# Attention's value products: a group over all four key blocks in one go, in place of two halves four steps apart

## The chip, the cores and the metric

The kernel runs on one core of one Trainium2 chip. The metric is the device time of one execution in microseconds (us), of which the median over the runs is taken.

## The reference

Three layers follow each other on x of 8 images by 512 tokens by 128 features: a Mamba block, then a mixture of experts, then attention, then the mixture of experts again. The change is in attention, which computes, cut to what matters:

```python
qk = x @ W_qk;  q, k = split(qk);  v = x @ W_v          # 8 heads, 64 wide (q, k) and 16 wide (v)
dots = einsum('bhid,bhjd->bhij', q, k) * SCALE          # per head 512 x 512
attn = softmax(dots + bias[None], axis=-1)              # bias by the clipped distance of j and i
out  = einsum('bhij,bhjd->bhid', attn, v)               # the value products
return out @ W_out + b_out
```

## The kernel before

All is in float32. An image's attention is done in `ST` = 32 steps. A step is one head and one block of 128 queries (`head_of`): its scores against all 512 keys are two records of 64x512 on TensorE (L1879, into `at_p_scores`, three banks; issued in pairs, two steps ahead). VectorE adds the band of biases and finds the row minimum (L2124, "bias(s)" below), ScalarE takes the exponential (L2011, "exp(s)"), TensorE turns the 128x512 probabilities by four 128x128 transposes (L1886, "turn(s)", into `at_p_probs_T`, two banks), and a copy puts them in `at_probs_T` (even steps VectorE L2133, odd steps ScalarE L1978, "take(s)").

Eight steps make a group `v` (4 heads of one half of the heads, two query blocks). For a group the value products (`values`, L1908) run on TensorE: for each of the 4 key blocks `j` and 4 heads `q` one product with a 128x32 weight (the 16 values, a one for the row sum, and zeros) against 128x256 probabilities, accumulated over `j` in `at_p_o_T`. The four heads write four groups of 32 partitions. Each product makes two records in the trace. `valued` is raised at the end of a group.

Nothing is planned at run time: each engine's queue is the order in which its block of the program is written. In each step TensorE issues the scores of steps s+2 and s+3 (even s), value products if the step has any, then `tail` (the output side of the image before: `turn_back`, L1917, L1930, L1936, and its router, L1298 in step 14, L1304 in step 15), turn(s), and then `head` (the input side of the next image: L1830 in step 16, projections L1836 in steps 19 to 28, the V projection L1842 in step 30). The first image has no tail, the last no head. The six images between run in a loop of three rounds of two. ScalarE's queue in an even step has exp(s), take(s-1), its tail and head; VectorE's has bias(s), take(s-2), its tail (router, layer norm) and head.

Of the kernel before, what the change touches and what calls it, by code (L numbers as in the profile page):

```python
# [16 lines left out]
TPB = T // P  # L17
# [1688 lines left out]
def attention(k, at):  # L1706
# [4 lines left out]
    NG = H // HG  # L1711
    ST = H * TPB
    VS = 2 * HG
    RING = 4
    SV = ST // VS
    k.begin_stage()
    with ExitStack() as c:
# [34 lines left out]
        turned_taken = [S("turned_taken0"), S("turned_taken1")]  # L1752
        valued, oT_ready = S("valued"), S("oT_ready")
# [9 lines left out]
        def use(slot, b, u):  # L1763

            head, tail = HEAD[slot], TAIL[slot]
            if isinstance(b, int) and b == -1:
                return u - tail + 1
            if isinstance(b, int) and b == B:
                return head - tail + (head + tail) * (B - 1) + tail + u + 1
            return head - tail + (head + tail) * b + u + 1  # L1770
# [5 lines left out]
        Q_USE, K_USE, V_USE, O_USE = (2, 4, 5, 6), (3, 3, 4, 5), 6, 2  # L1776
# [12 lines left out]
        def head_of(s):  # L1789

            gr, q = s // (ST // NG), s % HG
            it = s % (ST // NG) // VS * 2 + s % VS // HG
            return gr * HG + q, gr, q, it
# [23 lines left out]
        def _(pe):  # L1817
            k.from_one(pe, turned, valued)

            def mm_free(slot, b, u):  # L1820
                pe.wait_ge(mm_taken[slot], use(slot, b, u))

            def mm_there(slot, b, u):
                pe.wait_ge(mm_taken[slot], use(slot, b, u) + 1)
# [21 lines left out]
            def head(b, s):  # L1846

                if s == 16:
                    x_turn(b)
                elif s in (19, 23, 25, 27):  # L1850
                    p = (19, 23, 25, 27).index(s)
                    project(b, 0, Q_USE[p], p)
                elif s == 21:
                    project(b, 0, K_USE[0], H // 2)
                elif s in (24, 26, 28):
                    p = (24, 26, 28).index(s) + 1
                    project(b, 1, K_USE[p], H // 2 + p)
                elif s == 30:
                    project_v(b)

            def scores(b, par, s):

                if s == 0:
                    mm_there(0, b - 1, K_USE[0])
                elif s == 2:
                    mm_there(0, b - 1, Q_USE[1])
                    mm_there(1, b - 1, K_USE[1])
                elif s == ST // 2:
                    mm_there(0, b - 1, Q_USE[3])
                    mm_there(1, b - 1, K_USE[3])  # L1870
                for n in (s, s + 1):
                    if n >= SCB:
                        pe.wait_ge(biased, 1 + b * ST + n - SCB + 1)
                    elif not (isinstance(b, int) and b == 0):
                        before = ST - SCB + (n - ST % SCB) % SCB
                        pe.wait_ge(biased, 1 + (b - 1) * ST + before + 1)
                    hd, _, _, it = head_of(n)
                    half = slice(hd % 2 * DQK, (hd % 2 + 1) * DQK)
                    nc.tensor.matmul(psc[:, n % SCB, :], qT[par][half, hd // 2, it * P:(it + 1) * P],  # L1879
                                     kT[par][half, hd // 2, :], start=True, stop=True).then_inc(scored, 1)  # L1880

            def turn(b, s):
                pe.wait_ge(probs_ready, 1 + b * ST + s + 1)
                pe.wait_ge(turned_taken[s % 2], 1 + b * (ST // 2) + s // 2)
                for j in range(TPB):
                    mm = nc.tensor.transpose(ppt[:, s % 2, j * P:(j + 1) * P], pr[:, s % RING, j * P:(j + 1) * P],  # L1886
                                             k.ident[:])
                mm.then_inc(turned, 1)


            IDLE_BEFORE = {5: 3, 7: 3, 9: 3, 14: 14, 15: 3}
            VALUES_AT = {}
            for v, at in enumerate(((10, 14), (18, 22), (26, 30))):
                VALUES_AT.update({s: (v, 2 * j, 2 * j + 2) for j, s in enumerate(at)})

            def values(b, par, v, first, end):


                hd0, gr, _, it = head_of(v * VS)
                if first == 0:  # L1900
                    if v == 0:
                        mm_there(1, b - 1, V_USE)
                    for slot in range(2):
                        pe.wait_ge(turned_taken[slot], 1 + b * (ST // 2) + (v + 1) * (VS // 2))
                    pe.wait_ge(oT_ready, 1 + b * NG + gr)
                for j in range(first, end):
                    for q in range(HG):
                        mm = nc.tensor.matmul(pot[32 * q:32 * q + 32, it * P:(it + 2) * P], vv[par][:, j, hd0 + q, :],  # L1908
                                              prT[:, v % 2, q, j, :], start=j == 0, stop=j == TPB - 1)
                if end == TPB:  # L1910
                    mm.then_inc(valued, 1)

            def turn_back(b, gr):
                pe.wait_ge(oT_ready, 1 + (b - 1) * NG + gr + 1)
                mm_free(1, b, gr)
                for j in range(TPB):
                    mm = nc.tensor.transpose(pmm[:, 1, j * P:(j + 1) * P], oT[gr][:, j * P:(j + 1) * P], k.ident[:])  # L1917
                mm.then_inc(mm_done[1], 1)

            def tail(b, par, s):  # L1920

                if s in (1, 2):
                    values(b - 1, 1 - par, SV - 1, TPB // 2 * (s - 1), TPB // 2 * s)
                elif s in (3, 5):
                    turn_back(b, s // 2 - 1)
                elif s == 7:
                    mm_there(1, b, 1)
                    mm_free(0, b, 0)
                    for j in range(TPB):
                        mm = nc.tensor.transpose(pmm[:, 0, j * P:(j + 1) * P], on[:, j, :], k.ident[:])  # L1930
                    mm.then_inc(mm_done[0], 1)
                elif s == 9:
                    mm_there(0, b, 0)
                    mm_free(1, b, O_USE)
                    for j in range(TPB):
                        mm = nc.tensor.matmul(pmm[:, 1, j * P:(j + 1) * P], onT[:, j * P:(j + 1) * P], w_o,  # L1936
                                              start=True, stop=True)
                    mm.then_inc(mm_done[1], 1)
                elif s == 14:
                    rt.pe_turn(pe, b - 1)  # L1940
                elif s == 15:
                    rt.pe_logits(pe, b - 1)
                elif s == 20:
                    rt.pe_ranks(pe, b - 1)

            def core(b, par, first, last):
                for s in range(ST):
                    if s % 2 == 0 and s + 2 < ST:
                        scores(b, par, s + 2)
                    elif s % 2 == 0 and not last:  # L1950
                        scores(b + 1, 1 - par, s + 2 - ST)
                    if s in VALUES_AT:
                        values(b, par, *VALUES_AT[s])
                    if not first:
                        tail(b, par, s)
                    elif s + LATE < ST:
                        head(-1, s + LATE)
                    turn(b, s)
                    if not last:
                        head(b, s)  # L1960
# [15 lines left out]
        def _(act):  # L1976
# [37 lines left out]
            def take(b, s):  # L2014
                _, _, q, it = head_of(s)
                v = s // VS
                act.wait_ge(turned, 1 + b * ST + s + 1)
                if not (isinstance(b, int) and b * SV + v < 2):
                    act.wait_ge(valued, b * SV + v)
                copy(prT[:, v % 2, q, :, it % 2 * P:(it % 2 + 1) * P], ppt[:, 1, :].rearrange("p (j t) -> p j t", j=TPB)).then_inc(turned_taken[1], 1)  # L2020
# [50 lines left out]
        def _(dve):  # L2071
# [55 lines left out]
            def take(b, s):  # L2127
                _, _, q, it = head_of(s)
                v = s // VS
                dve.wait_ge(turned, 1 + b * ST + s + 1)  # L2130
                if not (isinstance(b, int) and b * SV + v < 2):
                    dve.wait_ge(valued, b * SV + v)
                V.tensor_copy(prT[:, v % 2, q, :, it % 2 * P:(it % 2 + 1) * P],  # L2133
                              ppt[:, 0, :].rearrange("p (j t) -> p j t", j=TPB)).then_inc(turned_taken[0], 1)
# [119 lines left out]
```

## Time and profile before

| | |
|---|---|
| median of 3 runs | 1220.24 us (1218.41 to 1222.12) |
| the profiled execution | 1221.0 us, its span 1219.2 us |
| TensorE busy | 1065.7 us (87%) |
| VectorE busy | 909.3 us (75%) |
| ScalarE busy | 840.4 us (69%) |
| value products in the trace (L1908) | 1024 records |

Attention takes the stretch from about 655 to 1110 us. The granted clock is given as a share of TensorE's full speed. A start in the rows is in us from the span's start; a matmul's own duration contains a modelled end that overlaps the next, so the time that a block takes is read as the difference of two starts.

### The profile page before, as it was taken

To read this page: it belongs to the slowest core of one execution; us is meant where nothing else is said; L and a number is where in the kernel's file an instruction comes from. 1 tells how busy PE (TensorE), PEld (TensorE's weight loads), DVE (VectorE), ACT (ScalarE), POOL (GpSimd) and SP (SyncE) were. 2 spreads that over 40 slices of the span, in tenths; PEclk is the share of its full clock that TensorE was granted. 3 is DMA by queue.
4 is the path that set the end of the run, shared out by engine and by line. 5 is a ranking of instruction groups with operands and counts; after the bars stand their busy time and mean duration, and the time that the engine had idled before them with its cause. 6 is when DMAs were issued, how large, how long until landed. Compare 5 with 4: busy or idle time off the path is not lost. (4 is left out here: it accounts for less than half of the span.)

```text
span 1219.2 us, 24911 instructions
## 1 busy us (share of the span) xinstructions
PE 1065.7 (87%) x7684; PEld 778.6 (64%) x7684; DVE 909.3 (75%) x1963; ACT 840.4 (69%) x1736; POOL 540.9 (44%) x363
## 2 busy tenths in 40 slices
PE   4876599988888888879969999989998999997897
PEld 3432488887888888769954454545454555546897
DVE  7797999989889889556637586848685867675465
ACT  4897799989889889346636675747574757562565
POOL 0389789999999999534420001010101010111344
PEclk9998699999999999899989999989999999998999
DMA  3001344444664564133311000000000000001331
GB/s 93 4 2 39 81 124 117 126 122 134 196 201 126 179 192 123 48 106 99 108 47 36 1 2 18 1 21 2 18 1 21 2 18 1 19 19 57 99 88 54
DMA packets 84444, 83.71 MB, mean 69 GB/s; under 512 B 23735, under 2 KB 62396, under 8 KB 84320
## 3 DMA queue, kind: packets, MB, share of 16 engines
q1 hardware_dynamic: 75440, 60.20, 18.2%
q0 software_dynamic: 5568, 12.66, 2.9%
q10 hardware_dynamic: 3312, 9.33, 2.5%
q8 instruction: 61, 1.00, 0.3%
q14 instruction: 63, 0.52, 0.1%
HBM read 65.73 MB, written 17.35 MB: 68 GB/s over the span
## 5 line engine op out<-in xcount | busy, mean ns | idle before, releaser
L1028 DVE TENSOR_TENSOR_SCAN h<-d_a,p_dbu 128x1024 f32<-128x1024 f32 x128 | 289.2, 2278 | 28.8 <-ACT d_a L794 16.2
L738 POOL TENSOR_TENSOR h<-h,c_rep 128x1024 f32<-128x1024 f32 x126 | 294.6, 2366 | 13.0 <-DVE h L1028 11.0
L2011 ACT ACTIVATE arena<-arena,at_min 128x512 f32<-128x512 f32 x256 | 183.7, 722 | 120.0 <-DVE at_min L2124 117.8
L2124 DVE CUSTOM_DVE_ANT_0 arena<-at_p_scores,arena 128x512 f32<-128x512 f32 x256 | 174.7, 685 | 80.8 <-PE at_p_scores L1879 45.0
L1346 POOL TENSOR_SCALAR r_row<-r_row 128x4 f32<-128x4 f32 x15 | 3.5, 231 | 462.0 <-DVEq L1252 462.0
L794 ACT ACTIVATE d_a<-arena,a_exp 128x511 f32<-128x511 f32 x256 | 169.7, 712 | 24.3 <-DVE h L1028 24.3
L1886 PEld LDWEIGHTS at_p_probs_T<-ident,arena 128*128 128x128 f32 x1024 | 112.5, 142 | 95.6 <-issue 68.5
L1879 PE MATMUL at_p_scores<-arena,at_q_T 64*128 64x512 f32 x512 | 159.6, 649 | 12.2 <-DVE at_min L2124 10.5
L786 ACT ACTIVATE b_du_T<-arena,b_T 128x256 f32<-128x256 f32 x392 | 166.6, 498 | 0.0
L1886 PE MATMUL at_p_probs_T<-ident,arena 128*128 128x128 f32 x1024 | 157.9, 283 | 4.1 <-ACT arena L2011 3.5
L918 PE MATMUL p_y_T<-ident,h 128*128 128x128 f32 x1024 | 134.9, 276 | 4.8 <-POOL h L738 4.2
L898 PE MATMUL p_dbu<-ident,b_du_T 128*128 128x128 f32 x784 | 112.2, 284 | 18.9 <-DVE h L1028 10.9
L918 PEld LDWEIGHTS p_y_T<-ident,h 128*128 128x128 f32 x1024 | 117.5, 143 | 7.3 <-POOL h L738 6.3
L2133 DVE COPY at_probs_T<-at_p_probs_T 128x512 f32<-128x512 f32 x128 | 88.1, 688 | 29.7 <-PE at_p_probs_T L1886 29.6
L898 PEld LDWEIGHTS p_dbu<-ident,b_du_T 128*128 128x128 f32 x784 | 90.2, 145 | 29.9 <-DVE h L1028 15.4
L1978 ACT ACTIVATE at_probs_T<-at_p_probs_T 128x512 f32<-128x512 f32 x128 | 75.6, 591 | 35.6 <-PE at_p_probs_T L1886 29.9
L1533 PE MATMUL f_p_h<-f_xg_T,f_w_cur 128*128 128x128 f32 x624 | 86.3, 283 | 6.1 <-DVE f_w_cur L1597 5.7
L1575 ACT ACTIVATE f_h_T<-f_p_h,f_w_cur 128x128 f32<-128x128 f32 x312 | 89.0, 375 | 3.4 <-PE f_p_h L1533 3.1
L1879 PEld LDWEIGHTS at_p_scores<-arena,at_q_T 64*128 64x128 f32 x512 | 43.2, 186 | 64.6 <-issue 43.3
L1545 PE MATMUL f_p_y<-f_w_cur,f_h_T 128*128 128x128 f32 x624 | 82.8, 276 | 1.1 <-issue 0.8
L1533 PEld LDWEIGHTS f_p_h<-f_xg_T,f_w_cur 128*128 128x128 f32 x624 | 77.0, 195 | 8.8 <-issue 7.0
L1545 PEld LDWEIGHTS f_p_y<-f_w_cur,f_h_T 128*128 128x128 f32 x624 | 75.8, 192 | 1.8 <-issue 1.7
(259 smaller groups left out, 1654.1 us busy)
## 6 DMA issues: line engine op xcount, KB each, us to landing
c_rep<-c_rows SPq DMA_DIRECT2D x128, 256.0 KB
f_row<-expert_rows SPq DMA_DIRECT2D x78, 129.0 KB
diag_b<-diag_rows SPq DMA_DIRECT2D x30, 256.0 KB, 4.3
arena<-in_w_all ACTq DMA_DIRECT2D x8, 578.0 KB
arena<-bias_by_distance ACTq DMA_DIRECT2D x8, 448.0 KB
x_tok<-in_x SPq DMA_DIRECT2D x4, 512.0 KB, 6.0
x_tok<-x_between SPq DMA_DIRECT2D x8, 256.0 KB, 2.8
diag_rows<-diag_b SPq DMA_DIRECT2D x4, 256.0 KB, 3.0
```

What stands on the lines that cost most here:

```text
L738: nc.gpsimd.tensor_tensor(h[:, n % HS, :, :], h[:, n % HS, :, :], cc, ALU.mult).then_inc(prod_done, 1)
L786: nc.scalar.activation(b_du[:, s % SR, j, :], du_T(b, j), ACT.Copy, scale=bT[:, one(b), j, s:s + 1].squeeze(1)).then_inc(scaled, 1)
L794: nc.scalar.activation(da[:, s % 2, ch, 1:], delta[:, one(b), ch, 1:].squeeze(1), ACT.Exp, scale=a_exp[:, ch, s:s + 1]).then_inc(da_ready, 1)
L898: mm = nc.tensor.transpose(dst, b_du[:, s % SR, j, ch * P:(ch + 1) * P], k.ident[:])
L918: mm = nc.tensor.matmul(p_yT[:, j, ch * P:(ch + 1) * P], h[:, n % HS, ch, j * P:(j + 1) * P], k.ident[:], is_transpose=SUM_BY_TRANSPOSE, s ...
L1028: nc.vector.tensor_tensor_scan(h[:, n % HS, :, :].rearrange("p c t -> p (c t)"), da[:, s % 2, :, :].rearrange("p c t -> p (c t)"), p_dbu[: ...
L1533: mm = nc.tensor.matmul(ph[:, r % R, f, :], w_cur[:, r % R, f * P:(f + 1) * P], xgT[:, r % R, :], start=True, stop=True)
L1545: mm = nc.tensor.matmul(py[:, r % YR, 0:D], ht[:, r % R, f, :], w_cur[:, r % R, FF + f * D:FF + (f + 1) * D], start=f == 0, stop=f == FC - 1)
L1879: nc.tensor.matmul(psc[:, n % SCB, :], qT[par][half, hd // 2, it * P:(it + 1) * P], kT[par][half, hd // 2, :], start=True, stop=True).then ...
L1886: mm = nc.tensor.transpose(ppt[:, s % 2, j * P:(j + 1) * P], pr[:, s % RING, j * P:(j + 1) * P], k.ident[:])
L2011: nc.scalar.activation(pr[:, slot, :], sc[:, slot, :], ACT.Exp, scale=-1.0, bias=mn[:, slot:slot + 1]).then_inc(probs_ready, 1)
L2124: V.tensor_tensor_reduce(sc[:, slot, :], psc[:, s % SCB, :], band[:, hd, w0:w0 + T], 1.0, 3.0e38, ALU.add, ALU.min, mn[:, slot:slot + 1]). ...
```

## The change

Before, a group's products ran in two halves of two key blocks each: in steps 10 and 14 for group 0, 18 and 22 for group 1, 26 and 30 for group 2, and in steps 1 and 2 of the next image for group 3. After, all four key blocks run in one go, in steps 14, 22, 30 and in step 2 of the next image. The number of products, their operands and their order within a group stay.

```diff
-            VALUES_AT = {}
-            for v, at in enumerate(((10, 14), (18, 22), (26, 30))):
-                VALUES_AT.update({s: (v, 2 * j, 2 * j + 2) for j, s in enumerate(at)})
-
-            def values(b, par, v, first, end):
+            VALUES_AT = {14: 0, 22: 1, 30: 2}
+
+            def values(b, par, v):
                 hd0, gr, _, it = head_of(v * VS)
-                if first == 0:
-                    if v == 0:
-                        mm_there(1, b - 1, V_USE)
-                    for slot in range(2):
-                        pe.wait_ge(turned_taken[slot], 1 + b * (ST // 2) + (v + 1) * (VS // 2))
-                    pe.wait_ge(oT_ready, 1 + b * NG + gr)
-                for j in range(first, end):
+                if v == 0:
+                    mm_there(1, b - 1, V_USE)
+                for slot in range(2):
+                    pe.wait_ge(turned_taken[slot], 1 + b * (ST // 2) + (v + 1) * (VS // 2))
+                pe.wait_ge(oT_ready, 1 + b * NG + gr)
+                for j in range(TPB):
                     for q in range(HG):
                         mm = nc.tensor.matmul(pot[32 * q:32 * q + 32, it * P:(it + 2) * P], vv[par][:, j, hd0 + q, :],
                                               prT[:, v % 2, q, j, :], start=j == 0, stop=j == TPB - 1)
-                if end == TPB:
-                    mm.then_inc(valued, 1)
+                mm.then_inc(valued, 1)
...
-                if s in (1, 2):
-                    values(b - 1, 1 - par, SV - 1, TPB // 2 * (s - 1), TPB // 2 * s)
+                if s == 2:
+                    values(b - 1, 1 - par, SV - 1)
...
                     if s in VALUES_AT:
-                        values(b, par, *VALUES_AT[s])
+                        values(b, par, VALUES_AT[s])
```

On TensorE, steps 10 and 14 of an image in the loop. Before, step 10 reads so (scores of steps 12 and 13, the first half of group 0, turn(10)):

```order
L1879 MATMUL at_p_scores<-arena,at_q_T 128x512
L1873 REGISTER_ALU
L1879 MATMUL at_p_scores<-arena,at_q_T 128x512
L1824 REGISTER_ALU
L1905 ISA
L1908 MATMUL at_p_o_T<-at_probs_T,arena 32x256 x8
L1884 REGISTER_ALU
L1886 MATMUL at_p_probs_T<-ident,arena 128x128 x4
```

After, the same step goes from the scores straight to the turn:

```order
L1879 MATMUL at_p_scores<-arena,at_q_T 128x512
L1873 REGISTER_ALU
L1879 MATMUL at_p_scores<-arena,at_q_T 128x512
L1884 REGISTER_ALU
L1886 MATMUL at_p_probs_T<-ident,arena 128x128 x4
```

In step 14 the block behind the scores is now of 16 products (it was L1908 with x8); L1298 behind it is the router's turn of the image before:

```order
L1879 MATMUL at_p_scores<-arena,at_q_T 128x512
L1873 REGISTER_ALU
L1879 MATMUL at_p_scores<-arena,at_q_T 128x512
L1824 REGISTER_ALU
L1900 ISA
L1903 MATMUL at_p_o_T<-at_probs_T,arena 32x256 x16
L1298 MATMUL at_p_mm<-ident,r_row 128x128 x4
```

The eight products and the wait ahead of them moved over two turns and two pairs of scores. The rest of the step is unchanged.

On TensorE, steps 0 to 2 of an image in the loop. Before: turn(0), a half of the group of the image before, turn(1), scores of steps 4 and 5, the other half, turn(2):

```order
L1886 MATMUL at_p_probs_T<-ident,arena 128x128 x4
L1904 ISA
L1905 ISA
L1908 MATMUL at_p_o_T<-at_probs_T,arena 32x256 x8
L1883 REGISTER_ALU
L1886 MATMUL at_p_probs_T<-ident,arena 128x128 x4
L1879 MATMUL at_p_scores<-arena,at_q_T 128x512
L1873 REGISTER_ALU
L1879 MATMUL at_p_scores<-arena,at_q_T 128x512
L1908 MATMUL at_p_o_T<-at_probs_T,arena 32x256 x8
L1884 REGISTER_ALU
L1886 MATMUL at_p_probs_T<-ident,arena 128x128 x4
```

After:

```order
L1886 MATMUL at_p_probs_T<-ident,arena 128x128 x4
L1883 REGISTER_ALU
L1886 MATMUL at_p_probs_T<-ident,arena 128x128 x4
L1879 MATMUL at_p_scores<-arena,at_q_T 128x512
L1873 REGISTER_ALU
L1879 MATMUL at_p_scores<-arena,at_q_T 128x512
L1899 ISA
L1900 ISA
L1903 MATMUL at_p_o_T<-at_probs_T,arena 32x256 x16
L1884 REGISTER_ALU
L1886 MATMUL at_p_probs_T<-ident,arena 128x128 x4
```

Turn(1) now stands directly behind turn(0), and both halves stand behind the scores of steps 4 and 5.

## Rows read from the trace of the kernel before

**Rows 1.** The chain of waits over the attention stretch (655 to 1110), shares by line.

```profile
by line: PE at_p_scores L1879 28.8%; PE at_p_probs_T L1886 23.8%; PE at_p_o_T L1908 11.3%; PE at_p_mm L1836 10.6%; issue 6.2%; ACT arena L2011 3.9%; DVE arena L2124 1.9%; DVE r_row L1207 1.7%; PE at_p_mm L1304 1.6%; PE at_p_mm L1842 1.4%; P
```

**Rows 2.** Busy us in one stretch, by engine (instructions); then granted clock, DMA share, GB/s.

```profile
715.00:775.00 60.00, 59.25 (x415) 31.11 (x413) 44.98 (x145) 38.88 (x66) 4.24 (x5) 1.00 0.03 10
```

**Rows 3.** Time line, end of attention; chain of waits, two turns (start, us, what).

```profile
1101.34 1.93 PE L1908 MATMUL at_p_o_T<-at_probs_T,arena 128*32 128x256 f32 x32 [0.73 <-DVE at_probs_T L2133]
1103.20 0.66 PE L1917 MATMUL at_p_mm<-ident,arena 128*128 128x128 f32 x4
...
796.63 0.59 PE at_p_probs_T L1886 x4
...
798.08 0.44 PE at_p_probs_T L1886 x4
```

**Rows 4.** Time line, steps 10 and 11 of a middle image.

```profile
834.99 0.87 DVE L1189 BATCH_NORM_STATS2 r_stats<-x_tok 128x6 f32 x4 [0.15 <-DVE x_tok L2154]
...
835.41 1.07 PE L1908 MATMUL at_p_o_T<-at_probs_T,arena 128*32 128x256 f32 x16
835.78 0.68 DVE L2124 CUSTOM_DVE_ANT_0 arena<-at_p_scores,arena 128x512 f32<-128x512 f32 x1
...
836.50 1.60 ACT L2011 ACTIVATE arena<-arena,at_min 128x512 f32<-128x512 f32 x2 [1.36 <-DVE at_min L2124]
...
837.27 0.66 PE L1886 MATMUL at_p_probs_T<-ident,arena 128*128 128x128 f32 x4 [0.21 <-ACT arena L2011]
```

**Rows 5.** Time line, steps 14 and 15 of the same image.

```profile
841.07 1.07 PE L1908 MATMUL at_p_o_T<-at_probs_T,arena 128*32 128x256 f32 x16
...
842.07 0.66 PE L1298 MATMUL at_p_mm<-ident,r_row 128*128 128x128 f32 x4
...
842.81 0.58 ACT L1278 ACTIVATE arena<-at_p_mm 128x512 f32<-128x512 f32 x1
...
843.44 1.06 PE L1304 MATMUL at_p_mm<-w_gate,arena 128*128 128x8 f32 x8 [0.28 <-ACT arena L1278]
```

**Rows 6.** Time line, steps 16 to 19 of the same image.

```profile
846.47 0.60 PE L1830 MATMUL at_p_mm<-ident,arena 128*128 128x128 f32 x4
...
847.07 0.66 PE L1886 MATMUL at_p_probs_T<-ident,arena 128*128 128x128 f32 x4
...
847.84 0.60 ACT L1978 ACTIVATE at_probs_T<-at_p_probs_T 128x512 f32<-128x512 f32 x1
...
848.72 1.07 PE L1908 MATMUL at_p_o_T<-at_probs_T,arena 128*32 128x256 f32 x16
848.82 0.72 ACT L2011 ACTIVATE arena<-arena,at_min 128x512 f32<-128x512 f32 x1
...
850.65 1.02 PE L1836 MATMUL at_p_mm<-arena 128*128 128x512 f32 x2
```

**Rows 7.** Time line, steps 0 to 2 of a middle image.

```profile
757.51 1.34 ACT L2011 ACTIVATE arena<-arena,at_min 128x512 f32<-128x512 f32 x2
757.88 1.07 PE L1908 MATMUL at_p_o_T<-at_probs_T,arena 128*32 128x256 f32 x16
...
758.88 0.65 PE L1886 MATMUL at_p_probs_T<-ident,arena 128*128 128x128 f32 x4
...
759.47 1.13 PE L1879 MATMUL at_p_scores<-arena,at_q_T 64*128 64x512 f32 x4
...
760.53 1.07 PE L1908 MATMUL at_p_o_T<-at_probs_T,arena 128*32 128x256 f32 x16
...
761.53 0.66 PE L1886 MATMUL at_p_probs_T<-ident,arena 128*128 128x128 f32 x4
```

**Rows 8.** Time line, the border where the loop branches back.

```profile
817.65 2.19 PE L1879 MATMUL at_p_scores<-arena,at_q_T 64*128 64x512 f32 x4 [5.54 <-DVE at_min L2124]
...
820.82 1.17 PE L1908 MATMUL at_p_o_T<-at_probs_T,arena 128*32 128x256 f32 x16
```

**Rows 9.** Time line, step 12 of the first image.

```profile
663.75 1.38 PE L1886 MATMUL at_p_probs_T<-ident,arena 128*128 128x128 f32 x8
```

## The prediction

> **What bounds the kernel now.** I first asked the chain of waits over the attention stretch for its shares by line [rows 1]: 28.8% of it is TensorE on the scores, 23.8% on the turns, 11.3% on the value products (L1908), and only some 10% stands under VectorE, ScalarE and "issue". So TensorE is nearly the bound, and a transfer is nowhere in it. The busy time of one stretch of 60 us in an image that is left undisturbed [rows 2] says the same: PE 59.25, DVE 44.98, ACT 38.88, at a granted clock of 1.00. The reader should see two things in this. TensorE has almost no idle time to fill, so work put late costs its whole length. And VectorE, three quarters busy on average, can't be idle everywhere: where the image's small router and layer-norm steps stand (steps 10 to 17), it can set the pace for a while, and TensorE work that stands there is free. So I then read the time line piece by piece, around each half of the value products, to see whether what follows it waited for TensorE or for something else.
>
> I call turn(s) the four transposes of step s, exp(s) ScalarE's exponential for it, take(s) the copy of its result.
>
> **The prices.** A half (8 products, 16 records) takes 1.00 us: one begins at 841.07 and what is behind it at 842.07 [rows 5], another at 757.88 and the turn behind it at 758.88 [rows 7]. All 16 products in one go are in the trace already, at the very end, where nothing stands between the halves: 1101.34 to 1103.20, 1.86 us [rows 3]. So joining two halves saves 0.14, and a step that held one half and now holds two grows by 0.86. Nearly the same 0.15 is at every change of form: a turn behind a score or value product takes 0.59, a turn behind a projection 0.44 [rows 3]. The Trainium skill (TensorEngine Tiling (Array Packing), Key Properties) says that changing the tiling mode drains TensorE; by it each joined pair loses one drain, and this case's 0.59 against 0.44 agrees. That rule taken alone speaks for the change; what it would give is the first rival below.
>
> Per image four pairs are joined: steps 10 and 14, 18 and 22, 26 and 30, and steps 1 and 2 of the next image. The last half keeps its place, so every later wait on `valued` is as before in order. The question is, pair by pair, whether the first half was on the path.
>
> **Steps 10 and 14.** In step 10 the half stands at 835.41 to 836.41. The turn(11) at 837.27 begins 0.21 after TensorE was free, released by ScalarE's exponential of 836.50, that by VectorE's bias of 835.78, and that stood behind the router's statistics of 834.99 on VectorE [rows 4]. None of these waits for the half. So with the half gone turn(10) comes 1.00 earlier, and turn(11) at the same 837.27: nothing is gained, TensorE's 0.21 of idle time becomes 1.21. In step 14 the doubled block adds 0.86, and what stands behind it is the router's turn of 842.07, ScalarE's copy of it at 842.81 (0.74 later) and the logits of 843.44 [rows 5]. ScalarE follows the shifted turn at once, so the logits come 0.85 later. The only slack up to the next pair is before turn(17): the turns before it start at 846.47 and take 0.44, so 0.16 of the time up to 847.07 is waiting [rows 6], and it is used up. Result at turn(17): +0.69. (If VectorE's cover in step 10 were not there, the 1.00 would be gained, and the pair would give -0.15.)
>
> **Steps 18 and 22.** Before, from turn(17) at 847.07 to the projection of 850.65 are 3.58 us, the half among them [rows 6]. Without it the pace is set by ScalarE: turn(17), its take at 847.84, a copy of the head, exp(19) at 848.82; that is 1.75 from turn(17), and another 0.77 from an exponential to its turn (836.50 to 837.27 in [rows 4]) and 0.59 for turn(19) make 3.11. So of the 1.00 only 0.47 comes back. At step 22 TensorE is behind heavy projections and bounds everything, so the 0.86 counts. Net +0.39.
>
> **Steps 26 and 30.** Most of the projections (L1836, 10.6% of the chain in [rows 1]) stand in steps 23 to 28, VectorE and ScalarE have no router work here, and the time line shows TensorE without a wait, so both halves are on the path: -1.00 and +0.86, net -0.14.
>
> **Steps 1 and 2 of the next image.** Before: half at 757.88, turn(1) at 758.88, scores 759.47, half 760.53, turn(2) at 761.53 [rows 7]. After: exp(1) begins at 757.51, so turn(1) can't begin before 757.51+0.77 = 758.28; scores at 758.87, 1.06 for them and 1.86 for the block give turn(2) at 761.79: +0.26. At two of the seven image borders, where the loop branches back, TensorE waits 5.54 us for VectorE ahead of the scores of 817.65; exp(1) is long done when they end, so turn(1) can take the half's place at 820.82 [rows 8], and both refills are saved: 2 x 0.15 = -0.30.
>
> **First and last image.** The first has no router work, so VectorE is lighter there; its two turns at step 12 are stretched to 1.38 by a wait of some 0.3 [rows 9], which ends earlier when the take ahead of it does, so that a half taken out is mostly gained: with the refills I put the whole image at -0.3, an estimate. The last has no projections: I take +0.86 for step 14 and a refill for each of the other two pairs, +0.6, again an estimate.
>
> **The sum.** Six middle images: 0.69+0.39-0.14 = 0.94, times 6 = 5.6. Borders: 5 x 0.26 - 2 x 0.30 = 0.7. First and last: 0.3. Together +6.6 us. The profiled execution took 1221.0, its span 1219.2, and the median of the runs is 1220.24, so the profiled one is 0.8 above it; 1227.6 for an execution like the profiled, 1226.8 as a median. Nothing else moves: no DMA, no instruction of the other engines, only the time at which TensorE gets to them. Cover that this leans on: VectorE's router steps (in step 10) and ScalarE's copies (in step 18). Behind the doubled block in TensorE's queue are the turn and then the next scores; VectorE's next bias stands behind the take of that turn, and I count that as part of the same shift.
>
> Bounds of the two unsure terms: steps 10 and 14 lie between -0.15 (all gained) and +0.86 (no slack used), seven times; steps 18 and 22 between -0.14 and +0.86, seven times. I take the values above since they follow rows of the very place.
>
> **Rivals.** (1) Faster: TensorE bounds everywhere, every joined pair gives its refill. 31 pairs (the last is joined already) by 0.15, and the second refill at the seven borders, give 31 x 0.14 + 7 x 0.15 = 5.4 less: 1214.8. For it: PE 59.25 of 60 busy. Against it: busy time counts modelled ends, and the wait at 837.27 has its releaser in the trace. It is decided at step 10: if turn(11) comes 0.8 or more earlier, this one holds. The skill's rule on the drain (same page and section) is what makes its price. Chance 0.13. (2) Same: only steps 10 and 14 lose (0.69), while 18 and 22 and the borders give their refills (-0.14 and -0.30) because ScalarE's exp(19) turns out to be early enough. Then an image gives 0.69-0.14-0.14-0.30 = +0.1, in all about +1: 1221. For it: ScalarE is only 65% busy, and the 0.47 rests on a chain of four steps whose phase shifts. Chance 0.23. (3) Slower still: the doubled block starves VectorE, whose bias of step s+1 is queued behind the take of step s-2, which waits for the turn behind the block; if that late bias reached TensorE as a new wait at each of steps 2, 14 and 22, an image would lose 3 x 0.86 - 0.14 = 2.4 and seven images 17: 1237. Against it: between turn(22) and turn(25) TensorE has two more turns at 0.59 and a pair of scores at 1.06 (759.47 to 760.53 in [rows 7]), 2.2 already, and projections besides, while the take, the bias (some 0.7 each, the bias in [rows 4]) and the 0.77 of the exponential are 2.2. Chance 0.10. The forecast itself has 0.50, with 1224 to 1230 as its own range; 0.04 is left to fetch stalls that move with the shorter program.
>
> **How the numbers follow.** A measurement of this kernel can tell 0.3% (3.7 us) from no change. The forecast and (3) are slower but for a small part of the forecast's low edge: 0.60. (2) and that edge: 0.26. (1) and stray: 0.14. The range from 1217 to 1232 leaves out (1), (3) and the ends of the others, about 2 in 10.
>
> **What would show it.** In the profile after: records of the value products in groups of 32 that take 1.86; TensorE idle for about 1.2 us before turn(11) in the six middle images, ended by ScalarE's exponential (right), or turn(11) earlier (rival 1); from the router's turn of step 14 to the logits still 1.37, but all of it 0.86 later as counted from the bias of step 10; a small new wait before turn(19), ended by the exponential; and some 0.9 us more from image to image. The forecast would be wrong if the time from turn(17) to the projection of step 19 fell by a full 1.0, or if VectorE showed new idle time before its bias of steps 17 or 25 with TensorE idle behind it.

## The result and the profile after

The changed kernel takes 1225.22 us (median of 14 runs, 1222.13 to 1229.24), the kernel before 1220.18 (14 runs on the same chips, 1217.49 to 1222.12). The ratio is 1.0048, with a 95% interval of 1.0039 to 1.0056. The changed kernel is slower: by 5.0 us as the difference of the medians, by 5.9 as the ratio, with 4.8 to 6.8 as the interval. Below, too, "+x by the ratio" is the ratio's excess over one times the median of the kernel before. The profiled execution took 1225.57, its span is 1223.4.

The busy time of the same undisturbed 60 us as in [rows 2], columns as there:

```profile
715.00:775.00 60.00, 56.86 (x391) 30.48 (x389) 43.85 (x141) 38.00 (x64) 4.22 (x5) 1.00 0.03 10
```

TensorE's busy time fell from 59.25 to 56.86, and the work done fell with it (391 records for 415), at the same granted clock. TensorE now stands idle. Where it does, the time line of the changed kernel shows in steps 10 and 11 of the middle image of [rows 4] (start, us, engine, line, what, and in brackets the idle time before it and its releaser):

```profile
836.01 1.13 PE L1879 MATMUL at_p_scores<-arena,at_q_T 64*128 64x512 f32 x4
...
836.65 0.87 DVE L1189 BATCH_NORM_STATS2 r_stats<-x_tok 128x6 f32 x4 [0.15 <-DVE x_tok L2148]
837.07 0.66 PE L1886 MATMUL at_p_probs_T<-ident,arena 128*128 128x128 f32 x4
837.44 0.67 DVE L2118 CUSTOM_DVE_ANT_0 arena<-at_p_scores,arena 128x512 f32<-128x512 f32 x1
...
838.16 0.72 ACT L2005 ACTIVATE arena<-arena,at_min 128x512 f32<-128x512 f32 x1 [1.37 <-DVE at_min L2118]
...
838.93 0.66 PE L1886 MATMUL at_p_probs_T<-ident,arena 128*128 128x128 f32 x4 [1.21 <-ACT arena L2005]
```

Turn(10) starts right behind the scores, 1.0 earlier than before, and then TensorE waits 1.21 where it waited 0.21: turn(11) is released by the exponential of 838.16, that by the bias of 837.44, that by VectorE being done with the statistics. The same chain as before, at the same distance.

Steps 14 and 15 of that image, to be held against [rows 5]:

```profile
842.73 1.93 PE L1903 MATMUL at_p_o_T<-at_probs_T,arena 128*32 128x256 f32 x32
...
844.60 0.66 PE L1298 MATMUL at_p_mm<-ident,r_row 128*128 128x128 f32 x4
...
845.29 0.60 ACT L1278 ACTIVATE arena<-at_p_mm 128x512 f32<-128x512 f32 x1 [0.73 <-PE at_p_mm L1298]
...
845.94 1.06 PE L1304 MATMUL at_p_mm<-w_gate,arena 128*128 128x8 f32 x8 [0.25 <-ACT arena L1278]
```

The block takes 1.87 (842.73 to 844.60), the half took 1.00. Everything behind it comes 0.87 later: counted from turn(11), the router's turn is at 5.67 now (844.60 less 838.93) and was at 4.80.

Steps 17 to 19, to be held against [rows 6]:

```profile
849.41 0.60 PE L1886 MATMUL at_p_probs_T<-ident,arena 128*128 128x128 f32 x4
...
850.13 0.59 ACT L1972 ACTIVATE at_probs_T<-at_p_probs_T 128x512 f32<-128x512 f32 x1
...
851.09 0.72 ACT L2005 ACTIVATE arena<-arena,at_min 128x512 f32<-128x512 f32 x1
...
851.87 0.66 PE L1886 MATMUL at_p_probs_T<-ident,arena 128*128 128x128 f32 x4 [0.21 <-ACT arena L2005]
852.36 1.02 PE L1836 MATMUL at_p_mm<-arena 128*128 128x512 f32 x2
```

From turn(17) to the projection are 2.95, before 3.58: of the 1.00 taken out, 0.63 came back. The new wait ahead of turn(19) is there, 0.21, ended by ScalarE's exponential.

The border between two images, against [rows 7]:

```profile
700.01 0.66 PE L1886 MATMUL at_p_probs_T<-ident,arena 128*128 128x128 f32 x4
...
701.00 0.66 PE L1886 MATMUL at_p_probs_T<-ident,arena 128*128 128x128 f32 x4 [0.33 <-ACT arena L2005]
...
701.59 1.13 PE L1879 MATMUL at_p_scores<-arena,at_q_T 64*128 64x512 f32 x4
...
702.65 1.93 PE L1903 MATMUL at_p_o_T<-at_probs_T,arena 128*32 128x256 f32 x32
...
704.52 0.66 PE L1886 MATMUL at_p_probs_T<-ident,arena 128*128 128x128 f32 x4
```

Turn(1) waits for exp(1), 0.33. From turn(0) to turn(2) are 4.51. Before, turn(0) stood at 757.29, and turn(2) of [rows 7] 4.24 behind it, so 0.27 less:

```profile
757.29 0.66 PE L1886 MATMUL at_p_probs_T<-ident,arena 128*128 128x128 f32 x4
```

A ruler for what follows: the time between the V projections (L1842) of two images that follow each other, the second and the third. Before, and in the changed kernel:

```profile
696.94 1.06 PE L1842 MATMUL at_p_mm<-arena 128*128 128x128 f32 x8
...
753.80 1.06 PE L1842 MATMUL at_p_mm<-arena 128*128 128x128 f32 x8
```

```profile
696.51 1.06 PE L1842 MATMUL at_p_mm<-arena 128*128 128x128 f32 x8
...
754.46 1.06 PE L1842 MATMUL at_p_mm<-arena 128*128 128x128 f32 x8
```

56.86 before, 57.95 after: +1.09 for an image with its border. This distance repeats within 0.05 from image to image of one execution (but for the two stalled borders), while whole executions of one kernel scatter by 4 us and more, so the experiments below are read by it as well as by their times. Each kernel has one trace. For a longer stretch the text uses "attention": from the first V projection to the last router's turn (L1298), 460.30 before and 465.24 in the changed kernel.

### The profile page after: what moved, and what is told of

Same layout as the page of the kernel before. It is cut to its first block and busy times, and to the rows that moved or that the text cites. A ratio compares the mean times of both kernels' runs of the same rounds, so it can differ in the third digit from the quotient of the medians.

```text
span 1223.4 us, 24911 instructions
## 1 busy us (share of the span) xinstructions
PE 1061.3 (87%) x7684; PEld 780.2 (64%) x7684; DVE 908.3 (74%) x1963; ACT 838.5 (69%) x1736; POOL 540.0 (44%) x363
```

## Experiments

**One group at a time.** Four kernels, each the kernel before with one pair joined late. Group 0, in step 14:

```diff
-            VALUES_AT = {10: (0, 0, 2), 14: (0, 2, 4), 18: (1, 0, 2), 22: (1, 2, 4), 26: (2, 0, 2), 30: (2, 2, 4)}
+            VALUES_AT = {14: (0, 0, 4), 18: (1, 0, 2), 22: (1, 2, 4), 26: (2, 0, 2), 30: (2, 2, 4)}
```

> Only group 0 is joined, in step 14; the other groups keep their halves. By the theory (the half of step 10 lay under VectorE's router work) the seven images with router work lose 0.69 us each and the first gains some 0.3: about +4.5 us over the kernel before, and an idle time of 1.2 us before turn(11). If TensorE bounded everywhere, eight refills of 0.14 would be gained: -1.1 us.

Measured: 1223.0 (7 runs) against 1218.44, ratio 1.0034 (1.0018 to 1.0050), so +4.1 by the ratio; attention grew by 4.15 in the trace. The ruler reads 57.51:

```profile
696.76 1.06 PE L1842 MATMUL at_p_mm<-arena 128*128 128x128 f32 x8
...
754.27 1.06 PE L1842 MATMUL at_p_mm<-arena 128*128 128x128 f32 x8
```

+0.65 an image. This one pair is most of the loss.

Group 1, in step 22:

```diff
+            VALUES_AT = {10: (0, 0, 2), 14: (0, 2, 4), 22: (1, 0, 4), 26: (2, 0, 2), 30: (2, 2, 4)}
```

> Only group 1 is joined, in step 22. By the theory ScalarE's chain from turn(17) over a take and a copy to exp(19) lets only 0.46 of the half's 1.00 come back at step 18, also where step 14 is not late: +0.4 us an image, about +3 in all, with a small wait before turn(19) ended by the exponential. The changed kernel showed +0.24 an image (0.63 came back), which would be +1.9. If both halves are on the path: -1.1 us.

Measured: 1221.42 (9 runs), ratio 1.0030 (1.0018 to 1.0043), +3.7 by the ratio. The ruler reads 57.13 (694.80 to 751.93), +0.27 an image, which is 1.9 in seven; attention grew by 1.94.

The wait before turn(19) is here too, without any lateness from step 14:

```profile
847.99 0.66 PE L1886 MATMUL at_p_probs_T<-ident,arena 128*128 128x128 f32 x4 [0.22 <-ACT arena L2009]
```

So the wait is there as forecast. The measured time is above what the trace explains; its interval reaches down to 2.2.

Group 3, in step 2 of the next image:

```diff
-                if s in (1, 2):
-                    values(b - 1, 1 - par, SV - 1, TPB // 2 * (s - 1), TPB // 2 * s)
+                if s == 2:
+                    values(b - 1, 1 - par, SV - 1, 0, TPB)
```

> Only group 3 is joined, in step 2 of the next image. By the theory, from one image's V projection to the router's turn of the next takes 0.26 longer at the five quiet borders (25.23 to 25.49), because turn(1) has to wait for exp(1); nothing else of the image moves. The changed kernel's stalled border lost 1 us to a lower granted clock while turn(1) ran earlier; if that is a rule and no chance, it is here too. If TensorE bounded: 0.30 shorter.

There is one execution, 1220.76 against a median of 1220.39, which tells nothing of 1 or 2 us. The ruler reads 57.10 (696.81 to 753.91), +0.24.

Group 2, in step 30:

```diff
+            VALUES_AT = {10: (0, 0, 2), 14: (0, 2, 4), 18: (1, 0, 2), 22: (1, 2, 4), 30: (2, 0, 4)}
```

> Only group 2 is joined, in step 30. Both halves are on the path: an image gets 0.14 shorter, from the router's turn to the V projection 31.63 to 31.49. If even here a longer block held back the others, it would be longer than 31.63.

Again one execution, 1219.18. The ruler reads 56.70 (695.68 to 752.38), -0.16, the refill and nothing else.

The four nearly add up: 0.65+0.27+0.24-0.16 = 1.00, and all four together give 1.09. The 0.09 between them is not explained.

**Place or length?** Group 0's first half moves to step 12, two turns ahead of the second, and nothing is joined:

```diff
+            VALUES_AT = {12: (0, 0, 2), 14: (0, 2, 4), 18: (1, 0, 2), 22: (1, 2, 4), 26: (2, 0, 2), 30: (2, 2, 4)}
```

> Group 0 keeps two halves, but the first moves from step 10 to step 12, the second stays in step 14: a change of place with no joined block and no refill saved. If the place is what costs (a free place in step 10 is given up for one on the path), each of seven images loses 1.00 less the 0.16 of waiting before turn(17): 0.84, about +5.5 in all with a first image that is little changed. If it were the length of a block in one piece that costs, with two turns between the halves nothing would be lost: within 1 us of before.

Measured: 1225.88 (4 runs), ratio 1.0063 (1.0046 to 1.0080), +7.7 by the ratio; attention grew by 6.21. The ruler reads 57.63, +0.77 an image:

```profile
696.13 1.06 PE L1842 MATMUL at_p_mm<-arena 128*128 128x128 f32 x8
...
753.76 1.06 PE L1842 MATMUL at_p_mm<-arena 128*128 128x128 f32 x8
```

The place costs. A half moved but not joined loses 0.12 more than one joined (0.77 for 0.65), about a refill. So the length of the block is not what costs at this pair. Seven times 0.77 is 5.4, and 5.5 was expected; what attention has beyond that lies mostly in the first image (+0.26) and at the two stalled borders (0.46 together).

**Is VectorE the cover?** Both kernels, before and changed, leave out most of VectorE's work in step 10: the attention output is added to 8 of the 128 features, and the router's statistics read 16 of them. They compute something else, and serve for the time alone:

```diff
-                    V.tensor_tensor(xb, pmm[:, 1, :].rearrange("p (j e) -> p j e", j=TPB), xb,
+                    V.tensor_tensor(xb[:, :, 0:8], pmm[:, 1, :].rearrange("p (j e) -> p j e", j=TPB)[:, :, 0:8], xb[:, :, 0:8],
...
-                self._step(V.bn_stats(self.stats[:, j, :], k.x[:, one(b * TPB + j), :].squeeze(1)))
+                row = k.x[:, one(b * TPB + j), :].squeeze(1)
+                self._step(V.bn_stats(self.stats[:, j, :], row[:, 0:16] if self.pool_tells else row))
```

> The kernel before with VectorE's step 10 cut: the attention output is added to only 8 of 128 features, and the router's statistics read 16 of 128. About 1.1 us of VectorE's work ahead of bias(11) is gone. TensorE waits only 0.21 before turn(11), so an image gains 0.2 there and perhaps 0.2 to 0.3 more at the later small waits: -2 to -4 us in all. This run is the base for the next.

> The changed kernel with the same cut in VectorE's step 10 (attention output added to 8 of 128 features, statistics over 16 of 128). By the theory the half of step 10 was free only because VectorE was late there; with that cover gone the idle time of 1.2 before turn(11) falls to some 0.1, and the changed kernel is only 0 to 2 us above the cut kernel before, in place of 5.8. If the cost is in the length of the block in step 14, the difference stays at 5 to 6 us.

Measured (10 runs each): the kernel before with the lighter step 10 takes 1219.27 (ratio to the full one 0.9985, 0.9972 to 0.9997), the changed one with it 1222.01 (ratio to the kernel before 1.0005, 0.9995 to 1.0016): 2.7 apart where the full ones are 5.0 apart. Less came off than planned: the bias ahead of turn(11) came 0.59 earlier, not 1.1. The changed kernel with the lighter step, step 10:

```profile
837.64 1.13 PE L1880 MATMUL at_p_scores<-arena,at_q_T 64*128 64x512 f32 x4
...
838.48 0.69 DVE L2119 CUSTOM_DVE_ANT_0 arena<-at_p_scores,arena 128x512 f32<-128x512 f32 x1
...
839.99 0.66 PE L1887 MATMUL at_p_probs_T<-ident,arena 128*128 128x128 f32 x4 [0.63 <-ACT arena L2006]
```

The bias is 0.84 behind the scores (1.43 in the full one), and TensorE's idle time went from 1.21 to 0.63. The ruler reads 56.50 for the kernel before with it (695.77 to 752.27) and 57.34 for the changed one with it (698.38 to 755.72), so the change costs 0.84 in place of 1.09. In attention it costs 4.16 in place of 4.94. So the traces confirm the direction, but less of it than the medians do (2.7 for 5.0), and the expected 0 to 2 was missed. What VectorE no longer does in step 10, TensorE gets back in the changed kernel (0.61 an image) more than in the one before (0.36). The wait shrank by 0.58 where the bias came 0.59 earlier, so the cover is VectorE's. That the whole 1.00 would come back with all of the cover gone was not shown.

**Is it one wait or a full stretch?** The changed kernel, nothing left out, with the router's statistics behind bias(11):

```diff
-                for stage, at in enumerate((10, 11, 12, 14, 17, 18, 19, 20, 21, 22, 23, 24)):
+                for stage, at in enumerate((11, 11, 12, 14, 17, 18, 19, 20, 21, 22, 23, 24)):
```

> The changed kernel with the router's statistics moved on VectorE from step 10 to step 11, behind bias(11), nothing left out. bias(11) and so turn(11) come 0.87 earlier. If that one wait is all that stands between TensorE and its gain, 0.87 comes back in each of 7 images, -6 us from the changed kernel, about 1219. If VectorE is full from step 10 on to step 13, the wait only moves on to the next bias: within 1.5 us of the changed kernel.

Measured: 1228.84 (4 runs), ratio 1.0071 (1.0055 to 1.0087) to the kernel before, so by the ratios some 3 us above the changed kernel, more than the 1.5 expected. The ruler reads 58.05 (695.87 to 753.92), only 0.10 above it; attention is 1.68 longer, 1.2 of it at one stalled border.

```profile
835.42 1.13 PE L1879 MATMUL at_p_scores<-arena,at_q_T 64*128 64x512 f32 x4
...
837.32 0.66 PE L1886 MATMUL at_p_probs_T<-ident,arena 128*128 128x128 f32 x4 [0.19 <-ACT arena L2005]
...
837.81 0.69 DVE L2118 CUSTOM_DVE_ANT_0 arena<-at_p_scores,arena 128x512 f32<-128x512 f32 x1
837.91 1.77 PE L1879 MATMUL at_p_scores<-arena,at_q_T 64*128 64x512 f32 x4
```

Turn(11) is 1.90 behind the scores now (2.92 in the changed kernel), a full microsecond earlier, and it bought nothing: the next scores are stretched from 1.13 to 1.77, because the bias that frees their bank starts only at 837.81. VectorE is full here, 5.25 us busy of the 5.40 from 835.80 to 841.20; the wait moves one bias on.

**Joining where it loses no cover.** Groups 1, 2 and 3 joined at their early places, group 0 left alone:

```diff
+            VALUES_AT = {10: (0, 0, 2), 14: (0, 2, 4), 18: (1, 0, 4), 26: (2, 0, 4)}
...
-                if s in (1, 2):
-                    values(b - 1, 1 - par, SV - 1, TPB // 2 * (s - 1), TPB // 2 * s)
+                if s == 1:
+                    values(b - 1, 1 - par, SV - 1, 0, TPB)
```

> Groups 1, 2 and 3 are joined at their early place (steps 18, 26 and 1 of the next image), group 0 keeps its halves in steps 10 and 14. By the theory no half loses a cover: in steps 18, 22, 26, 30 and 2 TensorE's work is on the path, so each joined pair gives its refill of 0.14: 22 pairs, -3 us, 1217. If a long block holds back VectorE and ScalarE by itself, whatever its place, this is no faster than before: 0 to +5 us.

Measured: 1219.02 (12 runs) against 1218.44, ratio 1.0000 (0.9990 to 1.0010). A miss: 3 us less were expected. The ruler gives -0.22 (695.19 to 751.83) where three refills make -0.42. TensorE has a wait behind the border that the two kernels below don't have:

```profile
706.68 0.66 PE L1886 MATMUL at_p_probs_T<-ident,arena 128*128 128x128 f32 x4 [0.27 <-ACT arena L2009]
```

So the border was left in halves:

```diff
+            VALUES_AT = {10: (0, 0, 2), 14: (0, 2, 4), 18: (1, 0, 4), 26: (2, 0, 4)}
```

> Only groups 1 and 2 are joined, early (steps 18 and 26); group 0 and the border keep their halves. The run with the border joined early too showed R to V 0.26 us shorter an image but lost it at the border and in the last image. By the theory each of 8 images gives two refills, 0.28, about -2 us over the kernel before. If a long block costs by itself, no faster than before.

Measured: 1220.69 (12 runs) against 1220.68, ratio 0.9998 (0.9989 to 1.0006), where 2 us less were expected. The ruler gives just the two refills, -0.28 (695.88 to 752.46).

The last image came out 0.9 longer: from the router's turn in its step 14 to the last router's turn are 38.48, before 37.60. So last, the same but for the last image:

```diff
+            VALUES_IN_LAST = {10: (0, 0, 2), 14: (0, 2, 4), 18: (1, 0, 2), 22: (1, 2, 4), 26: (2, 0, 2), 30: (2, 2, 4)}
...
+                    at = VALUES_IN_LAST if last else VALUES_AT
+                    if s in at:
+                        values(b, par, *at[s])
```

> Groups 1 and 2 joined early (steps 18 and 26) in seven images, not in the last, where the run with all eight gave back 0.9 us in waits of VectorE and ScalarE. By the theory 7 x 0.28, -2 us: 0.998 of the kernel before. If what was lost in the last image and at the stalled borders is chance of the fetches and not of the joins, the gain is smaller or none.

Measured: 1219.33 (12 runs) against 1220.39, ratio 0.9994 (0.9983 to 1.0005), again with 2 us less expected; the ruler reads 56.57 (695.00 to 751.57), the same -0.29. The two refills stand in both traces, but two or so microseconds in 1220 are at the edge of what the runs can tell: no version is shown to beat the kernel before.

## Why the prediction was right, and where its sizes were off

The sum was +6.6. The runs say +5.0 by the medians and +5.9 by the ratio, whose interval is 4.8 to 6.8. By the traces, attention from the first V projection (652.34 before, 652.05 after) to the last router's turn (1112.64 and 1117.29) grew by 4.94. So the size is near, and the paragraphs below say which terms made it so.

- **The prices.** The block in one go takes 1.87, the forecast said 1.86; the refill showed alone in step 30, 0.16 for 0.14. The Trainium skill (TensorEngine Tiling (Array Packing), Key Properties) says that changing the tiling mode drains TensorE. The 0.14 to 0.16 that a joined pair saves agrees, though no run here tells a drain from other costs between two blocks. The first rival had its price right and its premise, that TensorE bounds everywhere, wrong.
- **What a turn takes.** The prediction took 0.59 for a turn behind another form and 0.44 for one behind a projection. By the starts in the time lines of both kernels what follows the turn counts as well. Between two projections it takes 0.44 (before, 797.91 to 798.35), behind scores and ahead of a projection 0.49 (796.56 to 797.05), behind a projection and ahead of scores 0.53 (697.84 to 698.37), and 0.59 behind value products and ahead of scores (758.88 to 759.47). So the 0.15 has two parts: 0.05 for the form ahead of the turn, 0.10 for the form behind it. A turn behind a wait has the 0.05 too: turn(19) of the changed kernel took 0.49.
- **Steps 10 and 14.** +0.69 forecast, +0.65 measured with this pair alone. The 1.21 of idle time, its releaser and the 0.87 behind it came as written. Moving without joining, and the lighter step on VectorE, show that the place is the cause and VectorE's work the cover. The forecast's remark that without the cover the pair would give -0.15 stays an extrapolation.
- **Steps 18 and 22.** +0.39 forecast, +0.27 measured alone. The step that was off is the 3.11 from turn(17) to the projection: it is 2.95. The exponential came 1.68 behind turn(17) rather than 1.75, and turn(19), behind a wait and ahead of a projection, took 0.49 and not 0.59.
- **Steps 26 and 30.** -0.14 forecast, -0.16 measured.
- **The borders.** +0.26 forecast for a quiet one, +0.24 measured alone. The two stalled ones were put at -0.30 each. In the changed kernel they gave -0.1 and -0.8, with the group joined alone -0.9 and -0.1. Kernels whose border is written alike differ among themselves by as much: a stalled border is 5.78 to 6.28 longer than a quiet one in the kernel before, 5.13 and 6.51 with only group 0 joined, 6.98 and 5.54 with its half moved. So this term can't be read to better than about 1 us. The stall begins with VectorE, whose first bias at the first of the two starts 2.78 late in the kernel before (2.62 in the changed one), with no releaser in the profile; the cause of that is open:

```profile
815.19 0.69 DVE L2124 CUSTOM_DVE_ANT_0 arena<-at_p_scores,arena 128x512 f32<-128x512 f32 x1 [2.78 <-issue]
```

- **First and last image.** -0.3 forecast for the first, -0.14 measured (from 44.60 to 44.46 between its V projections); with group 0 joined alone it was -0.29, with group 1 alone +0.21, so the first image loses at steps 18 and 22 as well, where the forecast had a refill. The last was put at +0.6 and is at -0.25. Behind its border it is 0.75 later at the router's turn of step 14, forecast 0.86, and from there to the last router's turn 1.0 shorter (37.60 before, 36.60 after). The kernel before has a wait there that ends with ScalarE's copy; the copy stands 1.93 behind ScalarE's work before it, released by nothing on the core. The same copy in the kernel with only the border joined has 0.38:

```profile
1096.66 0.60 ACT L1978 ACTIVATE at_probs_T<-at_p_probs_T 128x512 f32<-128x512 f32 x1 [1.93 <-remote]
```

```profile
1095.10 0.60 ACT L1976 ACTIVATE at_probs_T<-at_p_probs_T 128x512 f32<-128x512 f32 x1 [0.38 <-PE at_p_probs_T L1886]
```

Of the four variants that are written like the kernel before from that turn on, and leave nothing out, two have the wait too (37.62 with group 0 joined, 37.61 with its half moved) and two don't (36.71 with the border joined, 36.71 with the last image left alone). So some 0.9 of the 1.0 comes and goes without the change, and the forecast of +0.6 would hold but for it. What brings it is open: the kernels have one trace each, and the forecast set only 0.04 aside for stalls that move.

Mis-sized, then, are the last image (0.85 too much, all of it that stall of the kernel before) and steps 18 and 22 (0.12 an image too much, 0.7 in all). Without the stall attention would have grown by about 5.8, an estimate from the 4.94 and the 0.9. A reading of [rows 1] was low too: the shares shown under VectorE, ScalarE and "issue" make 13.7%, not some 10%.

Of the rivals, "faster" fell with the first experiment. "Same", in which step 18 would give its refill, fell with the second. "Slower still" had VectorE starved behind the block; no idle time of that kind that reached TensorE appeared, and in an image of the changed kernel with a quiet border the only waits that TensorE's time line shows are those before turn(1), turn(11), the logits and turn(19). The early join at the border shows a relative of it: there the block stands ahead of the scores of steps 4 and 5, VectorE's bias on them comes later, and the wait of 0.27 shown above takes the refill again. That last reading is from one trace and was not tested by itself.

## What to carry to other kernels

Before work of the bounding engine is moved, ask of the place it leaves, not only of the place it goes to: if the next instruction there was released by another engine, the work was free as far as that release reaches, and moving it can cost up to its whole length. Here the 1.00 taken out of step 10 brought nothing, and 0.65 of the 0.87 added in step 14 was lost. An average of 99% busy on TensorE hid such a place in each of seven images. Joining blocks that change the array's form saves one refill a pair, about 0.15 us here, and pays only if neither place is a cover.

A wait's releaser is not enough either: taking the statistics out of the way of turn(11) moved the wait to the next scores, since VectorE had no room for some 5 us. Count the busy time of the releasing engine over the stretch until it is next idle.

## What was not expected of the hardware

The granted clock at the stalled border differs from kernel to kernel. In the stretch 817 to 823 of the changed kernel, and of the one with only the border joined, columns as in [rows 2]:

```profile
817.00:823.00 6.00, 4.34 (x14) 2.51 (x16) 3.38 (x9) 2.78 (x5) 0.00 (x0) 0.51 0.01 3
```

```profile
817.00:823.00 6.00, 5.56 (x32) 2.87 (x36) 3.18 (x12) 3.17 (x5) 0.00 (x0) 0.72 0.01 4
```

At 0.51, near the lower of TensorE's two levels (1.2 and 2.4 GHz), the scores of steps 2 to 5 and the turns of steps 0 and 1 ran at about half speed after TensorE had stood idle for 4.8 us. The second line is of two turns, the others are of two scores each, which take 1.06 at a granted clock of 1.00:

```profile
818.65 2.19 PE L1879 MATMUL at_p_scores<-arena,at_q_T 64*128 64x512 f32 x4 [4.77 <-issue]
820.78 1.97 PE L1886 MATMUL at_p_probs_T<-ident,arena 128*128 128x128 f32 x8
822.67 1.76 PE L1879 MATMUL at_p_scores<-arena,at_q_T 64*128 64x512 f32 x4
```

With the idle time nearly equal (4.97 in the other kernel) the clock came back sooner there, and from these scores to turn(2) took 6.63 for the 7.58 here. So the moment of its return was worth 0.95 at this border. What sets it, no run here shows. The 1.21 us of idle time ahead of turn(11) left the clock at 1.00.
